# The next unit's group average one group of channels later: an in-order matmul queue moved by one step

## The chip, the cores and the metric

The kernel runs on one core of a Trainium2 chip. The metric is the device time of one execution in microseconds (us), the median of several. The core's engines are called here as the profile calls them: PE (TensorE, matmuls), ACT (ScalarE), DVE (VectorE), POOL (GpSimd) and SP (SyncE, which here only issues DMAs). Each runs its own list of instructions strictly in order; they meet only at semaphores.

## The reference

Two layers of the same form are applied to `x` of shape (8, 512, 32, 32):

```
def layer(x, w, b):                       # w: (512, 512 + 25)
    f = group_norm(x, 32 groups)          # per image: mean and variance of 16 channels x 1024 pixels
    fn = f / max(norm over channels, 1e-12)
    vol[k] = sum over channels of shifted(fn, k) * fn,   k = 25 shifts of a 5x5 window
    return x + relu(w @ concat(f, vol) + b)
x = layer(x, w0, b0); x = layer(x, w1, b1)
```

## The kernel before

The work is cut into 16 units, one image of one layer each, in the order images 0 to 3 of layer 0, the same of layer 1, then images 4 to 7. After a hand-written start the units go through steady slots, `for k in range(STEADY, SLOTS)` with k from 3 to 17. A slot is the same loop on PE, ACT and DVE: a head, and then eight places j = 0 to 7. In slot k three units are under way:

- unit k + 1 is normalised: DVE has its statistics (`stats_tile`, `stats_done`, which ends at L832), PE multiplies them with a constant matrix that averages over the 16 channels of a group (`average`, L467, into `turn_ps`), DVE turns the averages into a scale and a shift (`unit_affine`, L838 to L859, with one square root on ACT in the middle, `deviations`, L679), ACT writes the normalised image twice (`norm_tile` L685 in half precision, `exact_tile` L692 in single), and DVE forms the rest (`low_tile` L866) and a halved copy (`half_tile` L872). Tiles 0 and 1 are done in the head, tiles 2 and 3 at places 1 and 2.
- unit k has its window correlations: PE makes them in two banks (`products`, L501 and L514, into `gram_ps`). For k above 3, bank 0 is made at place 7 of the slot before (`ahead`), bank 1 in the head. ACT takes each bank out (L699), SP sends it through DRAM to get it skewed, DVE makes norms and neighbours of it (`neighbours`, L895 to L915, with a square root on ACT, `lengths`, L706) at place 1, PE transposes them at place 5 (`turn`, L569), ACT takes them out (L712).
- the units k - 1 and k - 2 go through the convolution: at each place PE runs one group of channels (`channels`, 12 matmuls of 128x512, L579) and closes it with the correlation part (`volume`, L588); the first four places hold groups 4 to 7 of unit k - 2, the last four groups 0 to 3 of unit k - 1, whose group 0 gets its `volume` one place late. ACT rectifies the group (`rectified`, L721) and DVE adds it to `xs` (`added`, L951).

Three orders matter around the change. PE has four banks of `conv_ps`, so a group of channels waits until the group four places earlier has been rectified (`wait(pe, relu, GROUPS * u + g - 3)`). ACT's list in a slot is: bank 1 out of PSUM, the square root of unit k + 1, norm and exact of tiles 0 and 1, rectified of place 0, then at place 1 the square root of `lengths`, norm and exact of tile 2, rectified of place 1, at place 2 norm and exact of tile 3, rectified of place 2, and so on. DVE's list is: `unit_affine(k + 1)`, `correlation(k - 1)` (it waits for DMAs that POOL issued), low and half of tiles 0 and 1, added of place 0, `neighbours(k)`, low and half of tile 2, and so on; at place 7 it makes `stats_done(k + 2)`, whose average is the next slot's.

Two slots differ. In slot 3 both banks of products lie in the slot, bank 1 and its eviction behind place 0. In slot 4 (`W1_SLOT`) the weights of layer 1 are scaled (ACT, L664) and transposed (PE, L559) as well.

Of the kernel before, what the change touches and what calls it, by code (L numbers as in the profile page):

```python
# [58 lines left out]
def build(nc, x, w0, b0, w1, b1, out):  # L59
# [54 lines left out]
    with ctx:  # L114
# [120 lines left out]
        def valid(u):  # L235
            return 0 <= u < UNITS
# [45 lines left out]
        def ahead(u):  # L282

            return valid(u) and u > STEADY
# [5 lines left out]
        def group_of(k, j):  # L290

            u = k - 2 if j < HALF_AT else k - 1
            return (u, (j + 4) % GROUPS) if valid(u) and u > 0 else None
# [165 lines left out]
        def _(pe):  # L459
            pe.wait_ge(const_step, CONSTS)  # L460

            def average(u):

                pe.wait_ge(bn_step, BN_STEPS * (u + 1))
                if u > 0:
                    pe.wait_ge(gn_step, GN_STEPS * (u - 1) + 1)
                pe.matmul(turn_ps[:, 1, 0:2 * KT], avg[:, :], mv[:, :, :].rearrange("p t s -> p (t s)"),  # L467
                          start=True, stop=True).then_inc(group_avg, 1)
# [48 lines left out]
            def bank_products(u, n, t):  # L517

                for j in range(n * BANK_BLOCKS, (n + 1) * BANK_BLOCKS):
                    for s in range(SPLIT):  # L520
                        low_product(u, j, s, t)
                    for s in range(SPLIT):
                        last = high_product(u, j, s, t)
                return last
# [12 lines left out]
            def products(u, n):  # L537

                pe.wait_ge(low, KT * (u + 1))
                pe.wait_ge(halved, KT * (u + 1))  # L540
                pe.wait_ge(band_sb, BANKS * (u - 1) + n + 1)
                for t in range(KT):
                    last = bank_products(u, n, t)
                last.then_inc(gram, 1)

            def turn_weights(l, n):
                pe.wait_ge(w_scaled, KT * (l + 1))
                bank = w_turned_at(l, n)
                if l == 0 and n == KT:
                    pe.wait_ge(band_sb, 1)  # L550
                if l == 1:
                    pe.wait_ge(band_sb, BANKS * (W1_SLOT + 1))
                    if n in (2, 3):
                        pe.wait_ge(w_low, W_LOWS + n - 1)
                    if n == KT:
                        pe.wait_ge(rows_a, W1_SLOT + 1)
                for m in range(KT):
                    cols = slice(n * P, (n + 1) * P) if n < KT else slice(C, CI)
                    last = pe.transpose(bank[0:cols.stop - cols.start, m * P:(m + 1) * P],  # L559
                                        w_raw[l][:, m, cols], ident[:, :])  # L560
                last.then_inc(w_turned, 1)

            def turn(u):

                pe.wait_ge(rn_step, RN_STEPS * (u + 1))
                wait(pe, rows_a, u)
                both = nbr[:, :, :].rearrange("p (i h) n -> p i (h n)", h=HALVES)
                for i in range(FOLD):
                    last = pe.transpose(turn_ps[0:H_PART + NROWS, 0, i * P:(i + 1) * P],  # L569
                                        both[:, i, 0:H_PART + NROWS], ident[:, :])  # L570
                last.then_inc(turned, 1)

            def channels(u, g):

                l, m, n = unit_layer(u), g // 2, g % 2
                wait(pe, relu, GROUPS * u + g - 3)
                for t in range(KT):
                    for w, part in ((wh, 0), (wl, 0), (wh, 1)):
                        pe.matmul(conv_ps[:, g % 4, :], w[:, l, t, m * P:(m + 1) * P],  # L579
                                  opnd[:, u % RING, part, t, n * HALF:(n + 1) * HALF],  # L580
                                  start=(t == 0 and w is wh and part == 0), stop=False)

            def volume(u, g):

                l, m, n = unit_layer(u), g // 2, g % 2
                if g == 0:
                    pe.wait_ge(vol_in, 16 * VOL_PARTS * (u + 1))
                pe.matmul(conv_ps[:, g % 4, :], wvol[0:96, l, m * P:(m + 1) * P],  # L588
                          vol[0:96, u % 2, n * HALF:(n + 1) * HALF], start=False, stop=True).then_inc(conv, 1)
# [34 lines left out]
            for k in range(STEADY, SLOTS):  # L624
                if k == W1_SLOT + 1:
                    pe.wait_ge(w_low, W_LOWS + KT)
                if valid(k):
                    products(k, 1 if ahead(k) else 0)
                if valid(k + 1):
                    average(k + 1)  # L630
                for j in range(GROUPS):
                    if k == W1_SLOT and j in W1_TURNED_AT:
                        turn_weights(1, W1_TURNED_AT[j])
                    if k == W1_SLOT + 1 and j == HALF_AT:
                        pe.wait_ge(w_low, W_LOWS * LAYERS)
                    if j == TURN_AT and valid(k):
                        turn(k)
                    if j == AHEAD_AT and ahead(k + 1):
                        if k == W1_SLOT:
                            pe.wait_ge(w_low, W_LOWS + KT - 1)  # L640
                        products(k + 1, 0)
                    job = group_of(k, j)
                    if job is not None:
                        u, g = job
                        channels(u, g)
                        if g == HOLD:
                            for h in range(HOLD):
                                volume(u, h)
                        if g >= HOLD:
                            volume(u, g)  # L650
                    if j == 0 and valid(k) and not ahead(k):
                        products(k, 1)


        @block.scalar
# [413 lines left out]
```

## Time and profile before

| | us |
|---|---|
| median of 3 runs | 509.35 (508.88 to 510.59) |
| the profiled execution | 512.53 |
| its span, first to last instruction | 510.8 |
| PE busy | 443.5 (87%) |
| DVE busy | 370.6 (73%) |
| ACT busy | 287.1 (56%) |
| mean granted TensorE clock | 0.967 |

The span is the stretch that the profile shows; 1.7 us of the profiled execution lie around it. Busy time of PE counts overlapping matmuls once. The shares are averages over a start of some 107 us, the steady slots, and an end in which only the last units' channels are left.

### The profile page before, as it was taken

Reading aid. Unit: us, or ns where it says so; the run is one execution under the profiler, and the core shown is the slowest. Engines: PE = TensorE matmul, PEld = TensorE weight load, DVE = VectorE, ACT = ScalarE, POOL = GpSimd, SP = SyncE. Lnnn points to the kernel's source line nnn. Section 1 sums busy time; section 2 is a strip of 40 time slices with the busy share of each in tenths; the row PEclk is TensorE's granted clock in tenths of the full one; section 3 lists DMA queues with packets and bytes.
Section 4 is the critical chain, followed back from the end, with each engine's and each line's share of the span. In section 5 each row is a group of like instructions: output and inputs, shape, how many; then the busy total and the mean of one; then the engine's idle time right before and its main releaser. Section 6 shows DMA issues by size and latency. Waiting matters only on the chain.

```text
span 510.8 us, 13879 instructions
## 1 busy us (share of the span) xinstructions
PE 443.5 (87%) x5896; PEld 226.1 (44%) x5896; DVE 370.6 (73%) x871; ACT 287.1 (56%) x346; POOL 120.3 (24%) x171
## 2 busy tenths in 40 slices
PE   0457599197899999999999999999999999999996
PEld 0343345063454545454444435454545454444442
DVE  6788897676877978696868688797979786624422
ACT  1464265555568485665757574758576765813322
POOL 3505330131210313113031313131312122042300
PEclk9997889779799999999999999999999999999999
DMA  8261442523130363437657684232231316264422
GB/s 298 120 214 58 118 161 70 163 56 91 42 95 11 79 224 99 141 141 217 221 191 244 198 252 132 59 79 68 54 93 48 99 38 191 107 192 162 126 106 99
DMA packets 33988, 65.87 MB, mean 129 GB/s; under 512 B 11756, under 2 KB 21028, under 8 KB 33926
## 3 DMA queue, kind: packets, MB, share of 16 engines
q1 hardware_dynamic: 24134, 56.07, 33.4%
q0 software_dynamic: 9792, 8.92, 7.4%
q8 instruction: 46, 0.75, 0.6%
q14 instruction: 16, 0.13, 0.1%
HBM read 33.54 MB, written 28.87 MB: 122 GB/s over the span
## 4 chain that ended last, share of the span: by engine, by line
DVE 33%; PE 19%; ACT 16%; DMA 13%; issue 9%; SPq 5%; POOL 3%; DVEq 0%; ACTq 0%
PE conv_ps L579 16%; DVE stats L819 10%; ACT v L692 9%; DVE operands L866 7%; DVE xs L951 6%; ACT operands L685 5%; DMA skew<-band_dram 4%; DMA band_dram<-band 3%; DMA rn_far<-rows_dram 2%; DMA rows_dram<-rows 2%; DVE operands L872 2%; SPq L369 2%; PE conv_ps L588 2%; ACT act_out L721 1%; POOL v L444 1%
## 5 line engine op out<-in xcount | busy, mean ns | idle before, releaser
L579 PE MATMUL conv_ps<-operands,wh 128*128 128x512 f16 x1024 | 329.4, 384 | 3.5 <-ACT act_out L721 2.0
L579 PE MATMUL conv_ps<-operands,wl 128*128 128x512 f16 x512 | 196.4, 384 | 0.0
L579 PEld LDWEIGHTS conv_ps<-operands,wh 128*128 128x128 f16 x1024 | 102.0, 100 | 126.9 <-ACT act_out L721 6.3
L721 ACT ACTIVATE act_out<-conv_ps,bias,wdown 128x512 f32<-128x512 f32 x128 | 95.2, 771 | 79.1 <-PE conv_ps L588 79.1
L951 DVE TENSOR_TENSOR xs<-xs,act_out 128x512 f32<-128x512 f32 x128 | 85.6, 683 | 32.1 <-ACT act_out L721 32.1
L866 DVE TENSOR_TENSOR operands<-v,operands 128x1024 f16<-128x1024 f32 x64 | 81.6, 1276 | 37.3 <-ACT v L692 31.5
L685 ACT ACTIVATE operands<-xs,affine 128x1024 f16<-128x1024 f32 x64 | 92.9, 1457 | 19.9 <-DVE affine L859 19.9
L819 DVE BATCH_NORM_STATS2 stats<-xs 128x6 f32<-128x512 f32 x128 | 79.9, 681 | 2.5 <-DMA xs<-in_x_dram 2.4
L579 PEld LDWEIGHTS conv_ps<-operands,wl 128*128 128x128 f16 x512 | 50.6, 99 | 55.9 <-issue 2.2
L692 ACT ACTIVATE v<-xs,affine 128x1024 f32<-128x1024 f32 x52 | 68.5, 1317 | 0.0
L588 PE MATMUL conv_ps<-vol,wvol 96*128 96x512 f16 x128 | 47.2, 396 | 17.5 <-DMA vol<-corr_h 17.5
L323 POOL DMA_DIRECT2D vol<-corr_h x48 | 33.2, 698 | 118.8 <-DVE corr_h L888 118.6
L304 POOL DMA_DIRECT2D mirror<-rows_dram x14 | 9.4, 674 | 211.4 <-DMA rows_dram<-rows 211.4
L501 PE MATMUL gram_ps<-operands 128*32 128x108 f16 (+1 forms) x2048 | 49.8, 217 | 9.2 <-DVE operands L872 8.6
L501 PEld LDWEIGHTS gram_ps<-operands 128*32 128x32 f16 x2048 | 44.6, 101 | 22.2 <-issue 21.0
L514 PE MATMUL gram_ps<-operands 128*32 128x72 f16 (+1 forms) x2048 | 49.5, 202 | 0.0
L514 PEld LDWEIGHTS gram_ps<-operands 128*32 128x32 f16 x2048 | 45.3, 100 | 0.0
L699 ACT ACTIVATE band<-gram_ps 128x480 f32<-128x480 f32 x32 | 18.2, 569 | 35.8 <-PE gram_ps L514 35.6
L314 POOL DMA_DIRECT2D rn_far<-rows_dram x56 | 34.0, 748 | 0.0
L880 DVE TENSOR_TENSOR mirror<-mirror,rn_own 100x256 f32<-100x256 f32 x16 | 6.8, 424 | 32.8 <-DMA rn_far<-rows_dram 32.8
L706 ACT ACTIVATE nrm<-nsq 128x8 f32<-128x8 f32 x16 | 3.3, 207 | 48.4 <-DVE nsq L895 48.4
L444 POOL TENSOR_SCALAR v<-xs,affine 128x1024 f32<-128x1024 f32 x12 | 22.4, 1871 | 30.3 <-DVE affine L859 23.1
(75 smaller groups left out, 251.3 us busy)
## 6 DMA issues: line engine op xcount, KB each, us to landing
xs<-in_x_dram SPq DMA_DIRECT2D x32, 512.0 KB, 7.8
out_dram<-xs SPq DMA_DIRECT2D x32, 512.0 KB, 3.1
band_dram<-band SPq DMA_DIRECT2D x64, 120.0 KB, 2.9
skew<-band_dram SPq DMA_DIRECT2D x32, 222.5 KB, 3.0
vol<-corr_h POOLq DMA_DIRECT2D x48, 50.0 KB, 3.3
rows_dram<-rows SPq DMA_DIRECT2D x32, 65.8 KB
rows_dram<-rows SPq DMA_DIRECT2D x32, 63.3 KB
mirror<-rows_dram POOLq DMA_DIRECT2D x14, 110.9 KB, 2.5
```

Of the source, the lines that this page charges most:

```text
L314: eng.dma_start(rn_far[c:QPARTS:QUARTERS, 0:run], bass.AP(rows_dram, rn_row + c * QRUN, [[1, S], [PW, S], [1, run]])).then_inc(arrived, 16)
L323: eng.dma_start(vol[at:at + NS, k % 2, :].rearrange("s (q n) -> s q n", q=QUARTERS), corr_h[:, part, :]).then_inc(vol_in, 16)
L501: pe.matmul(window_at(j, s, top - y + 1, bottom - top), weights_at(u, j, s, t), bands_at(opnd[:, u % RING, 1, t, :], top, bottom - top, s) ...
L514: return pe.matmul(window_at(j, s, 1, n), weights_at(u, j, s, t), moving, start=False, stop=(t == KT - 1 and j % BANK_BLOCKS == BANK_BLOCK ...
L579: pe.matmul(conv_ps[:, g % 4, :], w[:, l, t, m * P:(m + 1) * P], opnd[:, u % RING, part, t, n * HALF:(n + 1) * HALF], start=(t == 0 and w ...
L588: pe.matmul(conv_ps[:, g % 4, :], wvol[0:96, l, m * P:(m + 1) * P], vol[0:96, u % 2, n * HALF:(n + 1) * HALF], start=False, stop=True).the ...
L685: act.activation(in_bands(opnd[:, u % RING, 0, t, :]), by_bands(xs[:, ring_slot(unit_batch(u)), t, :]), ACT.Identity, bias=affine[:, 1, t: ...
L692: act.activation(by_rows(v[:, t % 2, :]), in_rows(xs[:, ring_slot(unit_batch(u)), t, :]), ACT.Identity, bias=affine[:, 1, t:t + 1], scale= ...
L721: act.activation(in_rows(act_out[:, g % AOUT, :]), by_rows(conv_ps[:, g % 4, :]), ACT.Relu, bias=bias[:, l, m:m + 1], scale=wdown[:, l, m: ...
L819: last = dve.bn_stats(stats[:, t, h, :], xs[:, ring_slot(b), t, h * HALF:(h + 1) * HALF])
L866: dve.tensor_tensor(opnd[:, u % RING, 1, t, :], v[:, t % 2, :], opnd[:, u % RING, 0, t, :], ALU.subtract).then_inc(low, 1)
L951: dve.tensor_tensor(xt, xt, act_out[:, g % AOUT, :], ALU.add).then_inc(x_sum, 1)
```

## The change

The call of `average(k + 1)` moves from the head of the slot, directly behind the products, to behind place 0. Nothing is added or removed, and only PE's list changes.

```
-                if valid(k + 1):
-                    average(k + 1)
                 for j in range(GROUPS):
...
                     if j == 0 and valid(k) and not ahead(k):
                         products(k, 1)
+                    if j == 0 and valid(k + 1):
+                        average(k + 1)
```

It concerns the slots 3 to 14, twelve averages, of units 4 to 15. PE's list in slot 5, before: the end of the products (`gram_ps`), the average, the group of channels of place 0 (L579) with its correlation part (L588).

```order
L514 MATMUL gram_ps<-operands 32x36 x2
L467 MATMUL turn_ps<-mv,avg 128x8
L579 MATMUL conv_ps<-operands,wh 128x512
L579 MATMUL conv_ps<-operands,wl 128x512
L579 MATMUL conv_ps<-operands,wh 128x512 x2
L579 MATMUL conv_ps<-operands,wl 128x512
L579 MATMUL conv_ps<-operands,wh 128x512 x2
L579 MATMUL conv_ps<-operands,wl 128x512
L579 MATMUL conv_ps<-operands,wh 128x512 x2
L579 MATMUL conv_ps<-operands,wl 128x512
L579 MATMUL conv_ps<-operands,wh 128x512
L588 MATMUL conv_ps<-vol,wvol 128x512
```

The same place now:

```order
L514 MATMUL gram_ps<-operands 32x36 x2
L579 MATMUL conv_ps<-operands,wh 128x512
L579 MATMUL conv_ps<-operands,wl 128x512
L579 MATMUL conv_ps<-operands,wh 128x512 x2
L579 MATMUL conv_ps<-operands,wl 128x512
L579 MATMUL conv_ps<-operands,wh 128x512 x2
L579 MATMUL conv_ps<-operands,wl 128x512
L579 MATMUL conv_ps<-operands,wh 128x512 x2
L579 MATMUL conv_ps<-operands,wl 128x512
L579 MATMUL conv_ps<-operands,wh 128x512
L588 MATMUL conv_ps<-vol,wvol 128x512
L467 MATMUL turn_ps<-mv,avg 128x8
```

The average has moved behind the thirteen matmuls of place 0, and all that stands ahead of it and behind it keeps its order.

In slot 3 the call lands behind the second bank of products too. PE's list at the end of that bank, before, and behind it the group of place 1:

```order
L501 MATMUL gram_ps<-operands 32x3x36 x2
L501 MATMUL gram_ps<-operands 32x2x36 x2
L514 MATMUL gram_ps<-operands 32x2x36 x2
L514 MATMUL gram_ps<-operands 32x36 x2
L579 MATMUL conv_ps<-operands,wh 128x512
```

and now:

```order
L501 MATMUL gram_ps<-operands 32x3x36 x2
L501 MATMUL gram_ps<-operands 32x2x36 x2
L514 MATMUL gram_ps<-operands 32x2x36 x2
L514 MATMUL gram_ps<-operands 32x36 x2
L467 MATMUL turn_ps<-mv,avg 128x8
L579 MATMUL conv_ps<-operands,wh 128x512
```

There the average of unit 4 has moved past a group of channels and a whole bank of products.

## Rows read from the trace of the kernel before

**Rows 1.** The page: PE busy, and the granted clock by fortieths of the span.

```profile
PE 443.5 (87%) x5896; PEld 226.1 (44%) x5896; DVE 370.6 (73%) x871; ACT 287.1 (56%) x346; POOL 120.3 (24%) x171
...
PEclk9997889779799999999999999999999999999999
```

**Rows 2.** Waits: us in total, times, longest us.

```profile
PE turn_ps L467 <- DVE mv L832: 15.6, 12, 10.7
```

**Rows 3.** Windows: length, busy us (instructions) by engine, clock, DMA share, GB/s.

```profile
176.00:449.20 273.20, 265.42 (x3675) 133.09 (x3662) 213.92 (x519) 179.55 (x210) 60.21 (x96) 1.00 0.45 138
285.80:314.70 28.90, 26.90 (x380) 13.19 (x368) 22.29 (x58) 17.96 (x21) 6.67 (x12) 1.00 0.63 199
395.40:421.80 26.40, 26.21 (x384) 13.36 (x372) 21.76 (x53) 17.97 (x21) 6.17 (x11) 1.00 0.28 74
130.90:135.60 4.70, 4.70 (x13) 1.67 (x11) 4.70 (x8) 1.31 (x3) 0.00 (x0) 0.50 0.16 44
```

**Rows 4.** Timeline of slot 13: start, duration, engine, line [idle before, releaser].

```profile
395.41 0.20 PE L514 MATMUL gram_ps<-operands 128*32 128x72 f16 x2
395.80 0.39 PE L467 MATMUL turn_ps<-mv,avg 128*128 128x8 f32 x2 [0.19 <-DVE mv L832]
396.05 0.38 PE L579 MATMUL conv_ps<-operands,wh 128*128 128x512 f16 x1
397.06 0.20 ACT L679 ACTIVATE gstd<-gvar 128x4 f32<-128x4 f32 x1 [0.82 <-DVE gvar L845]
398.86 0.38 PE L579 MATMUL conv_ps<-operands,wh 128*128 128x512 f16 x1
403.85 1.23 DVE L866 TENSOR_TENSOR operands<-v,operands 128x1024 f16<-128x1024 f32 x1 [0.98 <-ACT v L692]
405.93 0.17 DVE L895 TENSOR_SCALAR nsq<-skew 128x8 f32<-128x8 f32 x1
408.80 0.77 ACT L721 ACTIVATE act_out<-conv_ps,bias,wdown 128x512 f32<-128x512 f32 x1
410.31 0.38 PE L579 MATMUL conv_ps<-operands,wh 128*128 128x512 f16 x1
412.01 1.45 ACT L721 ACTIVATE act_out<-conv_ps,bias,wdown 128x512 f32<-128x512 f32 x2
413.34 0.38 PE L579 MATMUL conv_ps<-operands,wh 128*128 128x512 f16 x1
421.80 0.20 PE L514 MATMUL gram_ps<-operands 128*32 128x72 f16 x2
```

**Rows 5.** Timeline of slot 9, PE at place 5.

```profile
305.65 0.61 PE L588 MATMUL conv_ps<-vol,wvol 96*128 96x512 f16 x2 [0.46 <-DMA vol<-corr_h]
```

**Rows 6.** Timeline of slot 3.

```profile
107.33 0.27 PE L514 MATMUL gram_ps<-operands 128*32 128x72 f16 x2
108.42 0.38 PE L579 MATMUL conv_ps<-operands,wh 128*128 128x512 f16 x1
111.14 0.20 ACT L679 ACTIVATE gstd<-gvar 128x4 f32<-128x4 f32 x1 [2.92 <-DVE gvar L845]
112.58 0.20 PE L514 MATMUL gram_ps<-operands 128*32 128x72 f16 x2
112.71 0.39 PE L579 MATMUL conv_ps<-operands,wh 128*128 128x512 f16 x1
127.43 0.17 DVE L895 TENSOR_SCALAR nsq<-skew 128x8 f32<-128x8 f32 x1 [2.97 <-DMA skew<-band_dram]
129.93 1.20 PE L569 MATMUL turn_ps<-ident,nbr 128*115 128x128 f32 x4 [6.02 <-DVE nbr L915]
```

**Rows 7.** Timeline of slot 4.

```profile
144.87 0.39 PE L467 MATMUL turn_ps<-mv,avg 128*128 128x8 f32 x2
148.00 0.19 ACT L679 ACTIVATE gstd<-gvar 128x4 f32<-128x4 f32 x1
167.06 0.60 PE L559 MATMUL turn_ps<-ident,xs 128*25 128x128 f32 x4 [1.84 <-ACT rows L712]
```

## The prediction

> **What bounds the kernel now.** I read the page first: PE is busy for 87% of the span, far ahead of DVE and ACT, and its clock stands at 9 tenths or more in every slice from the fifteenth on [rows 1]. Then the windows: the ten slots 5 to 14 (from one last correlation product to the next) take 273.20 us together, PE is busy for 265.42 of it, at a clock of 1.00; the light slot 13 takes 26.40 with 26.21 busy, slot 9, the longest, 28.90 with 26.90 busy [rows 3]. So in the light slots PE's own list sets the time, and it waits for others only a little.
>
> The view of the waits shows one such: PE stood idle before the averages for 15.6 us in all, twelve times, until DVE's `mv` (L832) came, once for 10.7 us [rows 2]. That one is the kernel's first average, which does not move; the rest is 4.9 us in eleven of the twelve that do, 0.19 us in slot 13 [rows 4]. This is what the move can win.
>
> Then the timeline of slot 13, for what hangs on the average [rows 4]. The average starts at 395.80. From there the reader can follow one chain without slack. ACT's square root starts at 397.06 (1.26 later; ACT had waited 0.82 us for it). DVE's `low_tile` 1 starts at 403.85, having waited 0.98 us for ACT's `exact_tile` 1. `added` of place 0 stands behind it on DVE, and the `nsq` of `neighbours` behind that (405.93, with no wait for its DMA). ACT's `lengths` and tile 2 wait for `nsq`, and the rectified of place 1 (408.80) stands behind tile 2, that of place 2 (412.01, 16.21 after the average) behind tile 3. PE at place 6 must have that one before it may reuse its bank: it ends 0.78 after its start (half of 1.45 for two, and a little of overlap), at 412.79, and PE starts place 6 at 413.34. That is 0.55 us of slack. At place 5 the rectified of place 1 ends at 409.57 and PE starts at 410.31: 0.74 us. PE's list binds, but a second chain, which begins at the average, runs half a microsecond behind it.
>
> **The change, part by part.** No instruction is added. The average takes PE 0.25 us before (395.80 to 396.05) and I take the same behind place 0; that term is nought.
>
> *Gain.* The `mv` that PE waited for is there long before, as place 0 lasts 2.81 us (396.05 to 398.86) [rows 4], and the eleven waits have a mean of 0.45. At most 4.9 us [rows 2].
>
> *Loss in the slots 5 to 14.* Measured from the last product's start, P, the average stood at P + 0.39 in slot 13 (395.41 to 395.80). Now place 0 starts at P + 0.13, as a group of channels does that follows products with no wait (112.58 to 112.71) [rows 6], and the average at P + 0.13 + 2.81 = P + 2.94. The chain hangs on it unchanged: rectified of place 2 starts 16.21 later and takes 0.78, and a semaphore's 0.03 (a small estimate from ACT's starts right at DVE's ends) makes 17.02, so PE starts place 6 at P + 19.96. Before it was P + 17.93 (413.34 less 395.41). From there to the last product of the next slot are 421.80 - 413.34 = 8.46 us [rows 4], which nothing of the chain shortens: two groups, two banks of products. So a slot now lasts 2.94 + 17.02 + 8.46 = 28.42 us. The slack of 0.55 and the won wait are in this number already. PE waits three times in it: for `turn`'s rows at place 5, for the rectified of place 1 there, and for that of place 2.
>
> This is a floor, not a surcharge. Slots whose chain is held by DMAs today already stand near it. The longest, slot 9 with 28.90, waits 0.46 us for the `vol` DMA behind place 5 [rows 3, 5]; that DMA starts with `correlation`, which waits for views of the slot before and not for the average, so I leave slot 9 as it is. Nine slots at 28.42 and one at 28.90 make 284.68, against 273.20 now: **+11.5 us**. From below this could be 8, if the chain finds more overlap in the slots that DMAs hold; from above 16, if in the six slots with heavier transfers 0.7 us of their own come on top of it.
>
> *Slot 3.* Here the average is moved past place 0 and the second bank of products. These take 4.16 us (108.42 to 112.58) and start at 107.33 + 0.13, so the average stands at 111.75 and the square root 1.26 behind it, at 113.01, against 111.14 before (DVE's four adds had held it up until then): 1.87 us later. ACT's eviction of bank 1 stands behind it; the skew DMA, `nsq` (127.43, it waited 2.97 for that DMA) and PE's `turn` (129.93, it waited 6.02) follow [rows 6]. PE gains nothing by being early here. **+1.9 us**, between 0 (the eviction's delay absorbed) and 3.7 (the whole shift of the average).
>
> *Slot 4.* The average moves from 144.87 by 2.81 to 147.68; its square root would come at 148.94 against 148.00. Then it had been held by the scaling of weights on ACT, so 1.9 of the delay is covered and 0.94 is not. Later in the slot PE waits 1.84 us for ACT's `rows` (167.06), so that ACT sets the time there [rows 7]. **+0.9 us**, between 0 and 2.8.
>
> Behind slot 14 there is no average. *Sum*, against the profiled execution's own time: 512.53 + 11.5 + 1.9 + 0.9 = 526.8. The median of the runs is 3.2 below that execution, so 509.35 + 14.3 = **523.7 us**, 2.8% slower.
>
> **A rule on the clock.** In slot 3 PE waited 6.02 us for `turn` and then ran at a clock of 0.50, 1.2 of 2.4 GHz, in the window behind it, 4.7 us long [rows 3, 6]; that costs 2.35 us. In slot 9, which had shorter waits, the clock was 1.00 throughout [rows 3], and the new waits, some 2.0 us per slot in three pieces (28.42 less the 26.40 of slot 13), are of slot 9's kind (28.90 less 26.90 busy). The rows say that the clock stays. If each of the slots 4 to 14 paid 2.35 us once, it would be 26 us more, 549.5.
> The Trainium skill, page "TensorE: Matmul & The Clock Gate", section "A second HAM failure mode: psum-queue depth-cycling", says that short idle spells between groups of matmuls, when PE cycles through PSUM banks, can make the clock swing between half and full. By that rule the sum would be the 549.5 worked out above; slot 9's clock does not agree with it.
>
> **The rivals.**
> - *The wait goes and nothing comes in its place* (faster). For it: PE's idle time before the averages is real, and DVE and ACT are busy for only 73% and 56%. Against: the 0.82 and 0.98 us in which ACT and DVE already wait within the chain; they are idle because of the average and not in reserve. It decides at a chain slack of 2.0 us before place 6; the trace has 0.55. It gives 509.35 - 4.9 = 504.4. Chance 0.05.
> - *The chain's delay and the won wait cancel* (no change): slots gain as much at the head as they lose at place 5 and 6. It needs a chain shorter by 1.2 us per slot than the rows have it, for instance `neighbours` or tile 2 starting ahead. 509.4. Chance 0.03.
> - *Transfers add to it*: the average's delay and the slower DMAs of the heavy slots (6 to 10 and 14) do not overlap, and each of the six pays 1.3 us more (the 2.0 us by which place 6 goes later, from P + 17.93 to P + 19.96, less the 0.7 that the bound above holds). 523.7 + 7.8 = 531.5. Against: in the chain they meet at one `nsq`, which waits for the later of the two only. Chance 0.06.
> - *The clock falls* after the new waits: 549.5. Chance 0.03.
> - *The forecast*: 523.7. Chance 0.83; its own range is 517 to 530.
>
> **How the numbers follow.** The forecast's range comes from the bounds: 8 instead of 11.5 and nothing in the slots 3 and 4 give 517.4; 16, and the upper bounds of 3.7 and 2.8 would give 531.9, which I do not expect together, so 530. The faster and the unchanged case and the two above lie outside it, 17 in 100; 516 to 530 therefore holds about 8 in 10. A measurement of this kernel can tell about 0.3% (1.5 us) from no change. Faster has the first rival's chance, 0.05; the same 0.03, and a little of the forecast's lower tail, 0.04 together; slower the rest, 0.91.
>
> **What the changed profile would show.** PE no longer idles before L467, or by under 0.1 us. The average starts about 2.9 us behind the last product. In every slot from 5 to 14 PE waits for DVE `nbr` before L569 and for ACT `act_out` before L579, at places 5 and 6, and slots are 28.4 us long, the light ones too. `nsq` no longer waits for the skew DMA in most of them. ACT's idle time before L679 grows by some 2 us a slot. PEclk stays at 9 in the steady slots. The prediction is wrong if the light slots stay below 27 us, if L579 shows no waits for L721, or if the clock shows digits of 5 to 8 behind slot 4.

## The result and the profile after

| | before | after |
|---|---|---|
| median, same chip (4 runs each) | 509.97 us | 524.61 us (523.7 to 526.97) |
| ratio of the runs | | 1.029, 95% interval 1.0242 to 1.0339 |
| the profiled execution, its span | 512.53, 510.8 | 525.2, 523.5 |
| PE busy | 443.5 (87%) | 445.2 (85%) |

The kernel is 14.6 us slower; between the two profiled executions it is 12.7 us. The forecast was 523.7.

The windows of the changed kernel, with the columns of [rows 3]: the slots 5 to 14, the light slot 13, and the stretch behind `turn` in slot 3.

```profile
177.80:461.80 284.00, 267.06 (x3676) 132.01 (x3664) 214.30 (x519) 179.34 (x210) 59.88 (x96) 1.00 0.43 133
405.10:433.50 28.40, 26.72 (x386) 13.20 (x372) 21.85 (x54) 17.93 (x21) 6.33 (x12) 1.00 0.26 70
131.50:136.40 4.90, 4.90 (x14) 1.82 (x13) 4.82 (x8) 1.38 (x3) 0.00 (x0) 0.50 0.15 42
```

The ten slots grew from 273.20 to 284.00 us at the same clock of 1.00, and the light slot from 26.40 to 28.40 with hardly more work in it. The waits of the changed kernel, as in [rows 2]:

```profile
ACT gstd L679 <- DVE gvar L845: 46.9, 16, 6.2
PE turn_ps L569 <- DVE nbr L915: 23.4, 12, 8.1
PE turn_ps L467 <- DVE mv L832: 10.6, 1, 10.6
PE conv_ps L579 <- ACT act_out L721: 4.8, 10, 0.5
```

and three of them in the kernel before:

```profile
ACT gstd L679 <- DVE gvar L845: 23.0, 15, 6.2
PE turn_ps L569 <- DVE nbr L915: 10.2, 4, 6.0
PE conv_ps L579 <- ACT act_out L721: 2.0, 5, 0.5
```

Only the kernel's first average still waits for `mv`: the 4.9 us are gone. In exchange PE waits for `nbr` twelve times instead of four (once in each of the slots 5 to 14, once in slot 3, once in the start) and for `act_out` ten times instead of five. The timeline of slot 13 of the changed kernel, which answers to [rows 4]:

```profile
405.11 0.20 PE L514 MATMUL gram_ps<-operands 128*32 128x72 f16 x2
408.06 0.29 PE L467 MATMUL turn_ps<-mv,avg 128*128 128x8 f32 x2
408.20 0.38 PE L579 MATMUL conv_ps<-operands,wh 128*128 128x512 f16 x1
409.18 0.20 ACT L679 ACTIVATE gstd<-gvar 128x4 f32<-128x4 f32 x1 [3.24 <-DVE gvar L845]
415.98 1.23 DVE L866 TENSOR_TENSOR operands<-v,operands 128x1024 f16<-128x1024 f32 x1 [0.99 <-ACT v L692]
418.06 0.17 DVE L895 TENSOR_SCALAR nsq<-skew 128x8 f32<-128x8 f32 x1
420.56 0.69 PE L569 MATMUL turn_ps<-ident,nbr 128*115 128x128 f32 x4 [1.18 <-DVE nbr L915]
421.73 0.39 PE L579 MATMUL conv_ps<-operands,wh 128*128 128x512 f16 x1 [0.48 <-ACT act_out L721]
424.15 1.41 ACT L721 ACTIVATE act_out<-conv_ps,bias,wdown 128x512 f32<-128x512 f32 x2
424.95 0.39 PE L579 MATMUL conv_ps<-operands,wh 128*128 128x512 f16 x1
433.50 0.20 PE L514 MATMUL gram_ps<-operands 128*32 128x72 f16 x2
```

The average stands 2.95 us behind the last product; the rectified of place 2 starts 19.04 behind it and PE starts place 6 at 19.84, where the forecast had 2.94, 19.15 and 19.96. The profile shows both of the slot's waits at place 5 (1.18 us for `nbr`, 0.48 for the rectified of place 1) and none at place 6; but place 6 starts 3.22 us behind place 5, where the kernel before took 3.03, and it starts just when the rectified of place 2 ends (424.15 and the 0.78 that one takes are 424.93, against 424.95). From there to the next last product it is 8.55. The slot is 28.39 us long. ACT's idle time before the square root has grown from 0.82 to 3.24.

From last product to last product, the slots 5 to 14 now last 28.41, 28.32, 28.38, 28.38, 28.42, 28.60, 28.38, 28.44, 28.39 and 28.31 us: the light and the heavy ones alike.

### The profile page after: what moved, and what is told of

It is laid out like the page before. It is cut to its first block, busy times and chain, and to the rows that moved or that the text cites. A ratio compares the mean times of both kernels' runs of the same rounds, so it can differ in the third digit from the quotient of the medians.

```text
span 523.5 us, 13879 instructions
## 1 busy us (share of the span) xinstructions
PE 445.2 (85%) x5896; PEld 224.2 (43%) x5896; DVE 371.4 (71%) x871; ACT 287.1 (55%) x346; POOL 120.0 (23%) x171
## 4 chain that ended last, share of the span: by engine, by line
PE 51%; DVE 18%; ACT 17%; issue 8%; DMA 4%; POOL 1%; SPq 0%; ACTq 0%; DVEq 0%
PE conv_ps L579 38%; ACT v L692 9%; PE gram_ps L501 5%; ACT operands L685 5%; DVE operands L866 4%; PE conv_ps L588 4%; PE gram_ps L514 2%; DVE stats L819 2%; ACT act_out L721 2%; DMA vol<-corr_h 2%; DVE xs L951 1%; DVE operands L872 1%; POOL v L444 1%; DMA xs<-in_x_dram 1%; ACT gstd L679 1%
## 5 line engine op out<-in xcount | busy, mean ns | idle before, releaser
L579 PE MATMUL conv_ps<-operands,wh 128*128 128x512 f16 x1024 | 330.4, 385 | 6.0 <-ACT act_out L721 4.8
L579 PE MATMUL conv_ps<-operands,wl 128*128 128x512 f16 x512 | 196.7, 384 | 0.0
L579 PEld LDWEIGHTS conv_ps<-operands,wh 128*128 128x128 f16 x1024 | 102.1, 100 | 133.8 <-ACT act_out L721 15.6
L951 DVE TENSOR_TENSOR xs<-xs,act_out 128x512 f32<-128x512 f32 x128 | 85.5, 683 | 32.4 <-ACT act_out L721 32.4
L579 PEld LDWEIGHTS conv_ps<-operands,wl 128*128 128x128 f16 x512 | 50.7, 99 | 53.0 <-issue 2.8
L588 PE MATMUL conv_ps<-vol,wvol 96*128 96x512 f16 x128 | 47.2, 396 | 16.6 <-DMA vol<-corr_h 16.6
L501 PEld LDWEIGHTS gram_ps<-operands 128*32 128x32 f16 x2048 | 43.5, 99 | 22.6 <-issue 21.2
L514 PE MATMUL gram_ps<-operands 128*32 128x72 f16 (+1 forms) x2048 | 48.4, 199 | 0.0
L514 PEld LDWEIGHTS gram_ps<-operands 128*32 128x32 f16 x2048 | 44.1, 99 | 0.0
L569 PE MATMUL turn_ps<-ident,nbr 128*115 128x128 f32 x64 | 12.2, 320 | 23.4 <-DVE nbr L915 23.4
L444 POOL TENSOR_SCALAR v<-xs,affine 128x1024 f32<-128x1024 f32 x12 | 22.3, 1868 | 30.2 <-DVE affine L859 23.1
L872 DVE TENSOR_SCALAR operands<-operands 128x1024 f16<-128x1024 f16 x64 | 29.1, 455 | 0.0
```

The lines of the kernel that those rows point to most:

```text
L501: pe.matmul(window_at(j, s, top - y + 1, bottom - top), weights_at(u, j, s, t), bands_at(opnd[:, u % RING, 1, t, :], top, bottom - top, s) ...
L514: return pe.matmul(window_at(j, s, 1, n), weights_at(u, j, s, t), moving, start=False, stop=(t == KT - 1 and j % BANK_BLOCKS == BANK_BLOCK ...
L872: dve.tensor_scalar(half[:, t, :], opnd[:, u % RING, 0, t, :], 0.5, None, ALU.mult).then_inc(halved, 1)
L951: dve.tensor_tensor(xt, xt, act_out[:, g % AOUT, :], ALU.add).then_inc(x_sum, 1)
```

## The experiments

Times are medians against the kernel before, measured beside them on the same chip: 508.1 us for runs 1 to 4, 510.97 for 5 to 8, 509.8 for 9 to 11. P is again the start of a slot's last correlation product. Slots are measured from P to the next P in one profiled execution.

**1. The steady slots alone.** The average moves in the slots 5 to 14 only (shown as an edit of the changed kernel).

```
+                if valid(k + 1) and k <= W1_SLOT:
+                    average(k + 1)
                 for j in range(GROUPS):
...
-                    if j == 0 and valid(k + 1):
+                    if j == 0 and valid(k + 1) and k > W1_SLOT:
                         average(k + 1)
```

> The average moves behind place 0 in the slots 5 to 14 alone; in slots 3 and 4 it stays in the head. Chain theory (the delay of the average runs through ACT's and DVE's lists to the rectified of place 2, for which PE waits at place 6): these slots are 28.4 us long each, as in the changed kernel, and slots 3 and 4 as before. +10.9 us, about 521. Rival (each average that stands between groups costs PE a fixed time of its own, 14.6 us over twelve): ten twelfths of it, about 522, but then with PE idle at the average and not at places 5 and 6.

Measured: 522.13 against 508.1, ratio 1.026 (1.0216 to 1.0304), 14.0 us (11.0 to 15.4 by the interval), more than the 10.9 expected. Nearly all of the loss is here. In all ten slots PE waits for `nbr` (1.1 to 1.2 us) and for `act_out` (0.4 to 0.5 us) at place 5 and not at the average, and they take 283.76 us together, as in the changed kernel. What was off is the term of comparison: the ten slots of run 2, which keep the old order, took 271.23 us in its profiled execution, 2.0 less than the 273.2 that I had from the kernel before. Against that the ten slots grow by 12.5.

**2. Slots 3 and 4 alone.** The same edit the other way round.

> Only the averages of slots 3 and 4 move. Chain theory: slot 3 1.8 us longer (from 37.4 to 39.2) by the later skew DMA and turn, slot 4 0.8 longer (from 31.2 to 32.0), the others as before: about 512.5. If PE's delay in slot 3 were absorbed: 510.5. Fixed cost per average: 2.4 us, which this run alone doesn't tell apart.

Measured: 511.4 against 508.1, ratio 1.0043 (1.0018 to 1.0069), 3.3 us (0.9 to 3.5 by the interval). The two together are 17.3 against the 14.6 of the whole change; the intervals of the three are wide enough for that. The parts did not come as expected, though: in its profiled execution slot 3 takes 37.11 us (39.2 expected) and slot 4 takes 33.73 (32.0 expected). Slot 4 of this run (wait and window), and below it the window at the same place of the changed kernel:

```profile
166.43 0.60 PE L559 MATMUL turn_ps<-ident,xs 128*25 128x128 f32 x4 [1.84 <-ACT rows L714]
167.60:171.10 3.50, 3.50 (x10) 1.27 (x9) 3.50 (x7) 1.03 (x3) 0.38 (x1) 0.54 0.18 56
170.05:173.55 3.50, 3.50 (x139) 2.11 (x137) 3.50 (x7) 1.82 (x4) 0.38 (x1) 1.00 0.20 61
```

Behind the same wait of 1.84 us the granted clock fell here and stayed at 1.00 in the changed kernel, whose slot 4 took 32.06 us. So 1.7 us of this slot's growth come with the clock and not from the chain.

**3. Two groups instead of one**, in the changed kernel.

```
-                    if j == 0 and valid(k + 1):
+                    if j == 1 and valid(k + 1):
                         average(k + 1)
```

> The average stands behind place 1, two groups of channels behind the products, in slots 3 to 14. Chain theory: the average at P + 5.75 instead of P + 2.94, so a slot lasts 5.75 + 17.02 + 8.46 = 31.2 us, ten slots 312.3 against 273.2 before; slot 3 4.7 and slot 4 3.7 us longer than before: about 557. Fixed cost per average: as the changed kernel, 524.6. Clock: more than 557, with digits of 5 to 8 in the granted clock of the steady slots.

Measured: 557.96 against 508.1, ratio 1.0961 (1.0888 to 1.1034). The windows of this kernel: the slots 5 to 14, and a stretch behind a wait at place 4; and one row of its timeline at the start of that stretch.

```profile
182.70:495.80 313.10, 281.02 (x3675) 136.14 (x3664) 214.05 (x519) 179.44 (x210) 59.86 (x95) 0.95 0.39 121
447.70:451.40 3.70, 3.64 (x10) 1.38 (x11) 3.25 (x11) 1.97 (x4) 0.00 (x0) 0.55 0.00 1
```
```profile
447.76 0.61 PE L579 MATMUL conv_ps<-operands,wh 128*128 128x512 f16 x1 [2.56 <-ACT act_out L721]
```

Ten slots last 313.1 us where the chain gave 312.3: the second group behind which the average waits costs one whole group, 2.8 us a slot. A fixed cost per average is refuted. The clock fell here (0.95 over the slots, 0.55 behind a wait of 2.56 us). In eight slots it fell behind the wait at place 4, and nothing was lost by it, for PE had to wait for the chain again at place 5; these, and slot 5, in which it did not fall, last 31.1 to 31.2 us, as long as the chain is. In slot 10 it fell one place later, with no wait behind it to hide that:

```profile
356.83 0.69 PE L569 MATMUL turn_ps<-ident,nbr 128*115 128x128 f32 x4 [1.21 <-DVE nbr L915]
358.00 0.39 PE L579 MATMUL conv_ps<-operands,wh 128*128 128x512 f16 x1 [0.48 <-ACT act_out L721]
358.00:362.00 4.00, 4.00 (x12) 1.60 (x13) 2.95 (x5) 4.00 (x5) 0.00 (x0) 0.61 0.01 2
```

That slot lasts 32.59 us, 1.4 more. So the clock is a cost here too, in one slot of ten. Slot 3 takes 39.81 us, 2.4 more than before and not 4.7, slot 4 takes 35.80, 4.6 more and not 3.7.

**4. The rectified of place 1 ahead of tile 2 on ACT**, in the changed kernel.

```
-                    if j in (1, 2) and valid(k + 1):
+                    if j in (1, 2) and j not in (1,) and valid(k + 1):
                         norm_tile(k + 1, j + 1)
                         exact_tile(k + 1, j + 1)
...
                         rectified(*job)
+                    if j in (1, 2) and j in (1,) and valid(k + 1):
+                        norm_tile(k + 1, j + 1)
+                        exact_tile(k + 1, j + 1)
```

> The changed kernel with one step on ACT's list moved: the rectified of place 1 stands ahead of norm and exact of tile 2, right behind the square root of lengths. Chain theory: PE no longer waits for ACT at place 5, but the rectified of place 2 still has the same work ahead of it on ACT and ends at the same time, so PE waits the same sum, at place 6; slots stay 28.4 us and the time 524.6, within 1.5. Rival (the waits of place 5 are what makes the slot longer): 0.5 us less in each of ten slots, 519.6.

Measured: 524.37, ratio 1.0305 (1.0266 to 1.0344), as the changed kernel. PE's two waits of the light slot in its timeline:

```profile
419.55 0.69 PE L569 MATMUL turn_ps<-ident,nbr 128*115 128x128 f32 x4 [1.17 <-DVE nbr L918]
423.97 0.39 PE L579 MATMUL conv_ps<-operands,wh 128*128 128x512 f16 x1 [0.71 <-ACT act_out L721]
```

The wait of 0.48 for ACT at place 5 is gone, and one of 0.71 stands at place 6. The slot is 28.4 us long as before. So with the rectified of place 1 out of the way that of place 2 alone holds the slot at its length, and the wait that the profile shows at place 5 was not the one that set it.

**5 and 6. The rectified of places 1 and 2 both ahead of the tiles**, in the kernel before (5) and in the changed one (6).

```
-                    if j in (1, 2) and valid(k + 1):
-                        norm_tile(k + 1, j + 1)
-                        exact_tile(k + 1, j + 1)
...
                         rectified(*job)
+                    if j in (1, 2) and valid(k + 1):
+                        norm_tile(k + 1, j + 1)
+                        exact_tile(k + 1, j + 1)
```

> Control: the kernel before, with ACT's list changed at places 1 and 2: the rectified of each place stands ahead of norm and exact of tiles 2 and 3. Chain theory: PE no longer waits for the rectified of places 1 and 2; in exchange tiles 2 and 3 come 0.7 and 1.4 us later, and with them DVE's list down to mv, which PE waits for at the head. Light slots about 0.7 us longer, all ten with the heavy ones 0.5 to 0.7: about 6 us more than before.

> The changed kernel with the same change of ACT's list as in the control. Chain theory: what carries the average's delay to PE is the rectified of place 2 behind tile 3; with it ahead, only turn (at P + 15.4) is left, a slot lasts at least 15.4 + 0.43 + 3.03 + 8.46 = 27.3 us, where the control's slots are 27.1 to 28.8 already. So the moved average costs only some 2 us (light slots and slot 3) against the control, not 14.6; about 10 us more than the kernel before. Rival (a cost of the late average on PE, or the delay of tiles for the products of place 7): against the control still 12 to 15 us.

Measured: 517.19 and 525.08 against 510.97, ratios 1.0115 (1.0087 to 1.0144) and 1.0269 (1.0242 to 1.0296). The control's 6.2 us is as forecast, if less evenly spread over the slots (26.2 to 30.3 us). The late average costs 7.9 us against it, neither the 2 of my theory nor the 12 to 15 of the rival; against the kernel before it is 14.1 where I had 10. Kernel 6: two averages in light slots, the `turn` of slot 8, two pieces of products, then what DVE waited for in the slots 6 and 8, and a window behind the `turn` of slot 6:

```profile
382.46 0.28 PE L467 MATMUL turn_ps<-mv,avg 128*128 128x8 f32 x2
410.00 0.28 PE L467 MATMUL turn_ps<-mv,avg 128*128 128x8 f32 x2
...
278.77 0.69 PE L569 MATMUL turn_ps<-ident,nbr 128*115 128x128 f32 x4 [2.39 <-DVE nbr L915]
318.08 0.23 PE L501 MATMUL gram_ps<-operands 128*32 128x108 f16 x4 [2.25 <-issue]
351.86 0.21 PE L501 MATMUL gram_ps<-operands 128*32 128x72 f16 x1 [1.50 <-issue]
...
218.37 0.17 DVE L895 TENSOR_SCALAR nsq<-skew 128x8 f32<-128x8 f32 x1 [0.74 <-DMA skew<-band_dram]
270.68 0.42 DVE L880 TENSOR_TENSOR mirror<-mirror,rn_own 100x256 f32<-100x256 f32 x1 [3.08 <-DMA rn_far<-rows_dram]
222.00:224.00 2.00, 2.00 (x6) 0.71 (x5) 1.88 (x3) 2.00 (x4) 0.00 (x0) 0.50 0.00 0
```

In the light slots the theory holds: 27.54 us by the averages, against a forecast of 27.3, and PE waits for `turn` only. The slots 6 and 8 took 30.04 and 30.44. There a DMA held DVE's list back, the skew DMA in slot 6 and the one for `correlation` (`rn_far`) in slot 8, so that `nbr` came 0.9 and 1.2 us later than in the light slots and PE waited 2.00 and 2.39 us for it; behind these waits the clock fell to 0.50, and the rest of the growth, some 1.6 us each, is there. In the slots 9 and 10 (29.90 and 29.41) PE stood still for 2.25 and 1.50 us in the middle of a bank of products with no releaser that the profile knows. In slot 4, too, the clock fell behind the wait for `rows`, as in run 2: it took 33.76 us, against 31.22 in the control. So what my 2 us left out is the clock, the DMAs and the stops. The control has some of each as well (its slots 7 and 11 ran at 0.94, and PE stopped for 1.36 and 0.58 us amid products), so how much of the 7.9 us the late average brings by each of them is not shown. Nor is the cause of the stops. The profile's view of the DMAs has a load of instructions (queue q8) within 1.8 us ahead of each of the four; no run tests whether that is it.

**7. Behind six matmuls of place 0** instead of behind all, in the kernel before.

```
-            def channels(u, g):
+            def channels(u, g, then=None):
...
                                   start=(t == 0 and w is wh and part == 0), stop=False)
+                    if then is not None and t == 1:
+                        average(then)
...
-                if valid(k + 1):
-                    average(k + 1)
...
-                        channels(u, g)
+                        channels(u, g, k + 1 if j == 0 and valid(k + 1) else None)
```

> The average stands inside place 0, behind six of its twelve matmuls, in slots 3 to 14. Chain theory: average at P + 0.13 + 1.29 = P + 1.42, so no slot is shorter than 1.42 + 17.02 + 8.46 = 26.9 us; light slots (26.4 to 26.6) get 0.3 to 0.5 longer, slots of 27.0 and more stay; PE's idle time before the averages (4.9 us) is gone, at places 5 and 6 it comes back. About 1.5 us more than before. Rival (the waits before the averages are lost time that a short move wins): 4.9 us less than before.

Measured: 512.12 against 510.97, ratio 1.0039 (1.0019 to 1.0059), 1.2 us in the medians. Its light slots last 26.8 to 26.9 us, where the chain gave 26.9.

**8. The statistics sooner**, in the kernel before.

```
-                        if j == 7:
+                        if j == 6:
                             stats_done(k + 2)
```

> The kernel before, average in its old place; DVE makes the statistics' end (aggregates and mv) at place 6 ahead of the added of place 6, not at place 7: mv 0.7 us sooner, so that PE hardly waits for it at the average. Chain theory: only the light slots are bound by PE and win the 0.2 to 0.3 us that they waited; the others are held by the chain and win nothing: 0 to 2 us less than before. Rival (the waits before the averages are lost time): 4.9 us less.

Measured: 510.69 against 510.97, ratio 1.0 (0.9978 to 1.0022). The time agrees, the reason given for it does not quite. Its timeline at the head of slot 13:

```profile
392.38 1.28 DVE L951 TENSOR_TENSOR xs<-xs,act_out 128x512 f32<-128x512 f32 x2
392.52 0.39 PE L467 MATMUL turn_ps<-mv,avg 128*128 128x8 f32 x2 [0.36 <-DVE mv L832]
393.58 0.16 DVE L838 COPY gmv<-turn_ps 128x8 f32<-128x8 f32 x1
```

PE still waits for `mv`, 0.36 us: two `added` now stand between `mv` and the copy of the average on DVE, so the copy comes 1.06 us behind the average, all of the chain is later, and DVE reaches the next `mv` later as well. Over the whole kernel the waits for `mv` outside the start come to 4.8 us, against 4.9 before. A wait was meant to be removed and was not.

**9. Behind three matmuls.** As 7, with `t == 0`.

> The average stands inside place 0, behind three of its twelve matmuls, in slots 3 to 14. Chain theory: average at P + 0.13 + 0.65 = P + 0.78, so the floor is 0.78 + 17.02 + 8.46 = 26.3 us, below every slot of today: nothing is lost, and the light slots win what they waited for mv beyond the floor, 0.1 to 0.2 each: within 1 us of the kernel before. Rival (the waits before the averages are lost time, 4.9 us): 3 to 4 us less.

Measured: 510.31 against 509.8, ratio 1.0019 (0.9995 to 1.0043). No gain, though in the slots 5 to 14 PE no longer waits for `mv` at all; the light slots last 26.2 to 26.6 us, against 26.4 to 27.0 in the profile of before, and in the heavy ones PE waits for `act_out` at place 5. The waits before the averages were not time to be won.

**10 and 11. A shorter chain**: `exact_tile` of tile 3 from ACT to POOL, in the kernel before (10) and the changed one (11). `last_exact` is a new function on POOL, the `tensor_scalar` of `exact_tiles` (L444) for tile 3, which waits for the `exact` of tile 2.

```
+                if k > EARLY and valid(k + 2):
+                    last_exact(k + 2)
...
                         norm_tile(k + 1, j + 1)
-                        exact_tile(k + 1, j + 1)
+                        if j == 1 or k == STEADY:
+                            exact_tile(k + 1, j + 1)
```

> The kernel before (average in the head), with the exact_tile of tile 3 on POOL instead of ACT in slots 4 to 14. Chain theory: the rectified of place 2 stands 1.25 us nearer to the average on ACT, so a slot's floor from the chain is 24.6 and PE's own list (26.1 to 26.2) binds in the light ones; slots with late DMAs are 1.25 shorter: ten slots 265 against 273 us, slot 4 1 us less: about 501. If ACT's length is no matter or POOL's tile (1.9 us) comes too late for low_tile 3: 509 or more.

> The changed kernel (average behind place 0) with the exact_tile of tile 3 on POOL. Chain theory: the rectified of place 2 is no longer the last link, that of place 1 is: PE starts place 5 at 2.94 + 13.81 = P + 16.7, place 6 3.03 later, so slots last 28.1 to 28.2 instead of 28.4: about 521.5, and the late average costs 20 us against the same kernel with the early one.

Measured: 507.97 against 509.8, ratio 0.9962 (0.9936 to 0.9987), and 520.66, ratio 1.0225 (1.0181 to 1.0268). Kernel 11 is where the chain puts it (521.5). Kernel 10 is faster than both kernels of the study, but by 1.8 us, not by 8. Groups of its profile, POOL's tile and the `added` on DVE (its L963 is L951 of before), one slot of its timeline, and POOL's same operation at the kernel's start (x2 is two instructions in that time):

```profile
L453 POOL TENSOR_SCALAR v<-xs,affine 128x1024 f32<-128x1024 f32 x11 | 28.4, 2584 | 57.4 <-ACT v L703 57.4
L963 DVE TENSOR_TENSOR xs<-xs,act_out 128x512 f32<-128x512 f32 x128 | 95.4, 759 | 32.1 <-ACT act_out L732 32.1
```
```profile
376.14 2.59 POOL L453 TENSOR_SCALAR v<-xs,affine 128x1024 f32<-128x1024 f32 x1 [6.15 <-ACT v L703]
377.64 1.59 DVE L963 TENSOR_TENSOR xs<-xs,act_out 128x512 f32<-128x512 f32 x1
389.24 0.39 PE L478 MATMUL turn_ps<-mv,avg 128*128 128x8 f32 x2 [0.32 <-DVE mv L844]
...
60.46 2.49 POOL L444 TENSOR_SCALAR v<-xs,affine 128x1024 f32<-128x1024 f32 x2
64.12 2.42 POOL L444 TENSOR_SCALAR v<-xs,affine 128x1024 f32<-128x1024 f32 x1 [1.17 <-DVE operands L878]
```

POOL's tile takes 2.58 us in place of the 1.9 I had put in, and one `added` per slot takes 1.59 in place of 0.68. The 1.9 was a mean that no instruction has: the group's twelve take 1.25 us each in six places (2.49 for two) and 2.3 to 2.7 in the other six. The cost has moved to DVE, whose `mv` PE waits for in nine of the ten slots; that it is the slower `added` that delays `mv` is read from the trace and not tested. In three of the heavy slots, besides, PE waited for the rectified of place 1 (0.19 to 0.48 us), which this edit does not bring nearer; I had worked out the last link of place 2 alone. As kernel 10 fell short, the late average costs 12.7 us against it, and not the 20 expected. Kernel 11's slots of 28.1 to 28.3 us also say how near the two last links lie in the changed kernel: with that of place 2 out of the way, that of place 1 binds 0.2 us sooner.

## Why the prediction was right, step by step

- *The gain, at most 4.9 us*: the waits went away, as said [rows 2]. That they were worth nothing by themselves was argued; run 9, in which they are gone from the slots 5 to 14, shows it. Run 8 does not, for it left them.
- *The floor of 28.42 us*: measured 28.31 to 28.44 in nine slots and 28.60 in one. Its three terms, 2.94, 17.02 and 8.46, were 2.95, 16.89 and 8.55 in slot 13. The sum came out, with two small errors of opposite sign: the chain is 0.13 shorter, since the square root follows the average by 1.12 us and not by 1.26, and PE's list behind it 0.09 longer. The average itself takes PE 0.14 us behind a group of channels (408.06 to 408.20), not 0.25; that is not a term of the sum. Runs 3 and 7 put the same formula to the test with the average 2.8 us later and 1.5 sooner, and it held: 31.2 in nine slots of ten, and 26.9 in the light ones.
- *The last link, place 2 of ACT*: shown by run 4. Run 11 shows that place 1 is only 0.2 us behind it, run 6 what is behind both in the light slots. The prediction had three waits in a slot, two at place 5 and one at place 6; the profile shows the first two, and the third only as the 0.19 us by which place 6 starts later behind place 5.
- *Slot 9 left at 28.90*: wrong. It fell to 28.42, the others' length. The wait for the `vol` DMA [rows 5] is gone. Ten slots grew by 10.85 us and not by 11.5.
- *Slot 3, +1.9*: 39.18 us from last product to last product (the first of them at 106.54) against 37.41, +1.77. In this the pair of profiles flatters the forecast: in the other profiles with the old order in slot 3 (runs 1, 5 and 8) it lasts 36.98, 37.95 and 36.92, and in others with the new one (runs 2, 4 and 6) 37.11, 38.25 and 37.37. The means of the four and four are 0.7 us apart, and the slot varies by more than that; what the move costs there is not settled. The rows that answer to [rows 6]:

```profile
110.97 0.39 PE L467 MATMUL turn_ps<-mv,avg 128*128 128x8 f32 x2
112.36 0.20 ACT L679 ACTIVATE gstd<-gvar 128x4 f32<-128x4 f32 x1 [4.90 <-DVE gvar L845]
128.10 0.17 DVE L895 TENSOR_SCALAR nsq<-skew 128x8 f32<-128x8 f32 x1 [3.12 <-DMA skew<-band_dram]
130.60 1.20 PE L569 MATMUL turn_ps<-ident,nbr 128*115 128x128 f32 x4 [8.08 <-DVE nbr L915]
```

- *Slot 4, +0.9*: 32.06 against 31.22, +0.84 (run 4: 32.11). The rows that answer to [rows 7]; PE's wait for `rows` is still 1.84, so ACT sets the time there as before:

```profile
149.81 0.20 ACT L679 ACTIVATE gstd<-gvar 128x4 f32<-128x4 f32 x1 [0.71 <-DVE gvar L845]
168.88 0.60 PE L559 MATMUL turn_ps<-ident,xs 128*25 128x128 f32 x4 [1.84 <-ACT rows L712]
```

- *The time*: 10.85 + 1.77 + 0.84 is 13.5; the profiled execution grew by 12.7, since its start, which the change does not touch, was 0.8 shorter (last product before slot 3 at 106.54, not 107.33). The medians differ by 14.6, against 14.3 forecast. That they are so near is in part luck. The prediction carried over the 3.2 us by which the profiled execution of the kernel before lay above its median, but the changed kernel's lies only 0.6 above. A chain that sets every slot leaves no room for a long slot: the ten slots take 284.03, 283.76 and 284.02 us in the changed kernel and in the runs 1 and 4, while in the old order they took 273.18 in one execution and 271.23 in another (run 2). Against the latter they grow by 12.8 us and not by the 11.5 of the sum, and slot 3 by less than its 1.9.
- *The clock*: it stayed at 1.00 in the ten slots with waits of 1.18 and 0.48 us in each. Runs 2, 3 and 6 show that it does fall: to 0.50 to 0.55 behind waits of 1.84, 2.56 and 2.00 us, and in slot 10 of run 3 to 0.61 behind 1.21 and 0.48. It does not go by the length of the last wait alone: behind the same 1.84 us in slot 4 it stayed at 1.00 in the changed kernel. The Trainium skill's rule on idle spells between groups ("TensorE: Matmul & The Clock Gate", "A second HAM failure mode: psum-queue depth-cycling") agrees with run 3 and not with the changed kernel.
- *`nsq` and its DMA*: the waits for the skew DMA fell from six to three, as forecast. The rival by which transfers add to the chain is refuted for the change by the heavy slots' 28.4; in the slots 6 and 8 of run 6, whose chain is shorter, transfers did hold `nbr` back.

## What to carry to other kernels

When a short instruction in a busy engine's list is awaited by others, its wait is not the price: measure the chain from it through the other engines back to the same engine, and compare it with that engine's own list. Here the chain had half a microsecond of slack in the light slots for a move of 2.55 us. The move brought all slots to one length, 28.4 us, whatever had bound them before: the light ones grew by 2.0, slot 9 even fell by 0.5; only the next place added its full 2.8 to nearly every slot. And a wait seen last (place 5) need not be the link that binds: take the next one down the list, and check with an edit that removes only one. Nor is one profiled execution the kernel: the same ten slots in the same order differed by 2.0 us between two of them, which is more than most terms of the sum.

## What the runs showed of the hardware

- An f32 matmul of 8 columns took PE 0.25 us behind small products and 0.14 us behind matmuls of 512 columns.
- Beside a POOL `tensor_scalar` of 128x1024 on SBUF a DVE `tensor_tensor` with both inputs in SBUF took 1.59 us instead of 0.68, in each of eleven slots of run 10. The POOL instruction itself took 2.58 us there, as against 1.25 for the fastest of the same form at the kernel's start. The Trainium skill, "SBUF — State Buffer", section "Who interferes with whom", says that such a `tensor_tensor` contends with POOL's reads; the run agrees with it.
- The granted clock fell to half behind the same 1.84 us wait of PE in one kernel (run 2, slot 4: 1.7 us lost) and stayed at 1.00 in another (the changed one).
- PE stood still for 2.25 and 1.50 us amid products in run 6, and for 1.36 and 0.58 us in run 5, with no semaphore awaited; no run explains it.
